# Second expert stage: weighted rows added into the output by an accumulating scatter

## What is computed

```python
x = x + 0.5 * ffn(layernorm(x), gate_w, gate_up_w, down_w)
x = x + mamba(layernorm(x), ...)
x = x + 0.5 * ffn(layernorm(x), gate_w, gate_up_w, down_w)
# ffn: 8 experts, F = 512, the 2 best of each token
probs = softmax(x @ gate_w.T); topw, sel = top_k(probs, 2); topw = topw / sum(topw)
out = sum over the 2 experts e of topw[e] * ((up_e(x) * gelu(gate_e(x))) @ down_e.T)
```

## Time and profile before

| | |
|---|---|
| three timed runs | 457.85, 460.02, 460.93 us; median 460.02 |
| span of the profiled execution | 459.4 us |
| PE busy | 404.0 us, 88% |
| DVE, ACT, POOL busy | 307.4, 240.0, 277.8 us |
| get: issue on POOL; issue to landing (median) | 1034 ns; 2.6 us |
| put: issue on POOL; issue to landing (median) | 1024 ns; 2.3 us |
| granted clock of TensorE, 328 to 441 us | 1.00 of full speed |

### The profile page before, as it was taken

How to read it: one execution, slowest core, us unless ns; L and a number is a source line. 1 busy time by engine, 2 the same in 40 slices (tenths; PEclk the granted TensorE clock), 3 DMA queues, 4 the chain that set the end, 5 groups by cost and what they waited for, 6 DMA issues and landing times.

```text
span 459.4 us, 9998 instructions
## 1 busy us (share of the span) xinstructions
PE 404.0 (88%) x2636; PEld 316.4 (69%) x2637; DVE 307.4 (67%) x761; ACT 240.0 (52%) x575; POOL 277.8 (60%) x262
## 2 busy tenths in 40 slices
PE   8779999999995998989979889984799999999940
PEld 6359999999994343434335346671499999999930
DVE  4824555555554967999989999999455555555516
ACT  4535444444434656686765867434454444444404
POOL 2167777777433252688685787765377777776330
PEclk9769999999997799999979999987699999999985
DMA  7942111112103200000000000001111111112026
GB/s 262 374 158 82 49 50 45 45 44 44 31 21 93 93 0 0 2 0 1 0 0 0 0 1 0 1 1 53 57 53 44 47 44 51 45 44 37 22 55 227
DMA packets 11964, 25.03 MB, mean 54 GB/s; under 512 B 3485, under 2 KB 4260, under 8 KB 11936
## 3 DMA queue, kind: packets, MB, share of 16 engines
q1 hardware_dynamic: 6944, 15.38, 9.5%
q0 software_dynamic: 4992, 9.32, 7.4%
HBM read 17.34 MB, written 8.26 MB: 56 GB/s over the span
## 4 chain that ended last, share of the span: by engine, by line
PE 65%; DVE 13%; ACT 7%; DMA 5%; issue 4%; POOL 4%; SPq 0%; POOLq 0%; ACTq 0%; DVEq 0%
PE ps L835 30%; PE ps L860 15%; PE ps L970 7%; DVE ring_space L1344 3%; DMA ring_space<-expert_rows 2%; ACT shared L705 2%; DVE stats L1097 2%; PE ps L830 2%; ACT ps L697 2%; POOL shared L486 2%; PE ps L957 2%; PE ps L951 2%; PE ps L903 1%; DMA xg<-xn_rows,get_i 1%; POOL rstd L398 1%
## 5 line engine op out<-in xcount | busy, mean ns | idle before, releaser
L835 PE MATMUL ps<-xT,w_now 128*128 128x128 f32 x1248 | 154.1, 277 | 0.8 <-ACT xT L574 0.7
L835 PEld LDWEIGHTS ps<-xT,w_now 128*128 128x128 f32 x1248 | 147.3, 194 | 1.4 <-ACT xT L574 1.1
L1226 DVE TENSOR_TENSOR hidden<-ps,hidden 128x256 f32<-128x256 f32 x156 | 58.9, 419 | 94.6 <-PE ps L835 94.6
L591 ACT ACTIVATE hidden<-ps 128x256 f32<-128x256 f32 x156 | 51.4, 381 | 111.2 <-PE ps L835 111.1
L434 POOL DMA_INDIRECT expert_rows<-ysb,put_i x78 | 79.9, 1024 | 46.5 <-DVE ysb L1234 30.1
L426 POOL DMA_INDIRECT xg<-xn_rows,get_i x78 | 80.6, 1034 | 45.1 <-issue 21.2
L486 POOL TENSOR_TENSOR shared<-ring_space,shared 128x512 f32<-128x512 f32 x64 | 81.9, 1287 | 35.5 <-DVE ring_space L1344 29.6
L860 PE MATMUL ps<-w_down,hidden 128*128 x624 | 82.1, 275 | 0.0
L970 PE MATMUL ps<-shared,consts 128*128 128x512 f32 x128 | 71.7, 644 | 7.6 <-POOL shared L486 7.4
L860 PEld LDWEIGHTS ps<-w_down,hidden 128*128 128x128 f32 x624 | 75.7, 192 | 0.2
L705 ACT COPY shared<-ps 128x512 f32<-128x512 f32 x64 | 37.6, 587 | 35.5 <-DVE ring_space L1344 18.2
(11 more groups left out here) (161 smaller groups left out, 410.6 us busy)
## 6 DMA issues: line engine op xcount, KB each, us to landing
w_gate_up<-in_experts SPq DMA_DIRECT2D x8, 512.0 KB, 8.6
xn_rows<-xn SPq DMA_DIRECT2D x8, 256.0 KB, 4.0
w_down<-in_experts SPq DMA_DIRECT2D x1, 2048.0 KB, 11.9
ring_space<-expert_rows SPq DMA_DIRECT2D x4, 512.0 KB, 5.9
xg<-xn_rows,get_i POOLq DMA_INDIRECT x78, 2.6
expert_rows<-ysb,put_i POOLq DMA_INDIRECT x78, 2.3
x<-in_x_rows SPq DMA_DIRECT2D x4, 256.0 KB, 4.5
ring_space<-expert_rows SPq DMA_DIRECT2D x4, 256.0 KB, 3.5
```

The lines of the kernel that those rows point to most:

```text
L591: nc.scalar.activation(gelu[:, slot % 2, half], ps[:, GATE_BANK[slot % 2], half], ACT.Gelu).then_inc(gelu_done, 1)
L835: m = pe.matmul(ps[:, bank, f * P:(f + 1) * P], w_now[:, slot % W_SLOTS, first + f * P:first + (f + 1) * P], xT[:, slot % X_SLOTS, :], sta ...
L1226: dve.tensor_tensor(hact[:, slot % H_SLOTS, half], ps[:, UP_BANK[slot % 2], half], gelu[:, slot % 2, half], ALU.mult).then_inc(hact_done, 1)
```

## The change

In the second stage alone:

- x after the Mamba block is stored at once to `out` (four stores on SP), which has grown to 7040 rows: the 2048 tokens, then one spare row for each of the 39 * 128 slots.
- The stored normalised rows have 130 columns instead of 128 (`xw`, `ROW`): columns 128 and 129 are the token's two weights. POOL makes `ldiff` group by group and the weights in two halves (`weights`), ACT runs its Exp in two halves, and SP waits for a half's weights before it stores the half's two groups. `normalise(2, 3)` comes after `row_ids(1)` and the second Exp.
- get(t) brings the weights with the rows and waits for `take_weight(t - 6)`, a new DVE instruction after `h_act`, which picks the row's weight into `slot_w`. `y_copy` multiplies by it.
- put(t) is an accumulating scatter into `out`. Filling rows go to their spare rows.
- A token may stand in two tiles of different experts, so puts are held apart: SP (`allow_puts`) lets put(t) go when `y_copy(t)` is done, the scatter of tile t - 2 has landed and, where tile t begins an expert, that of tile t - 1 has too. put(t) follows get(t + 8) instead of get(t + 10).
- DVE makes `add_i`, `not_second` and `starts_i` (`add_index`, eight instructions) ahead of its tile steps.
- The load of `expert_rows`, the scaling, the two additions and the six stores of x at the end of the second stage are gone. The first stage keeps them.

```diff
-PUT_AFTER = RING + TURN_AHEAD + DOWN_AFTER
+PUT_AFTER = RING + TURN_AHEAD + DOWN_AFTER, RING + DOWN_AFTER
+ROW = D + TOPK
+OUT_ROWS = T + NT * P
...
+            def landed(t):
+                return 16 * (PER_SLOT[t % RING] + t // RING + 1)
+            def allow_puts():
+                sp.wait_ge(add_index_ready, 1)
+                sp.wait_ge(base_stored, 16 * GROUPS)
+                for t in range(NT):
+                    if t >= 1:
+                        start = sp.value_load(starts_i[0:1, t:t + 1], min_val=0, max_val=16)
+                    sp.wait_ge(y_ready, NT + t + 1)
+                    if t >= 2:
+                        sp.wait_ge(scattered[(t - 2) % RING], landed(t - 2))
+                    if t >= 1:
+                        sp.wait_ge(scattered[(t - 1) % RING], start + (landed(t - 1) - 16))
+                    sp.sem_inc(may_put, 1)
...
+                        sp.wait_ge(out_added, g + 1)
+                        sp.dma_start(out[0:T].rearrange("(p c) d -> p c d", p=P)[:, grp(g), :], x[:, grp(g), :]
+                                     ).then_inc(base_stored, 16)
...
+                    if l:
+                        sp.wait_ge(weights_ready, g // 2 + 1)
+                    sp.dma_start(rows[:, grp(g), :], (xn, xw)[l][:, grp(g), :]).then_inc(xn_stored[g], 16)
...
+            def weights(h):
+                v = slice(2 * h * GC, 2 * (h + 1) * GC)
+                pool.wait_ge(e2_ready, h + 2)
+                chain(pool.tensor_scalar(den[:, v], e2[:, v], 1.0, None, ALU.add))
+                chain(pool.tensor_tensor(den[:, v], den[:, v], neg_one[:, v], ALU.pow))
+                chain(pool.tensor_tensor(xw[:, v, D], halves[:, v], den[:, v], ALU.mult))
+                pool.tensor_tensor(xw[:, v, D + 1], xw[:, v, D], e2[:, v], ALU.mult
+                                   ).then_inc(weights_ready, 1)
...
+                    if t >= RING and l == 1:
+                        pool.wait_ge(weight_taken, t - RING + 1)
...
+                    if l:
+                        pool.wait_ge(may_put, t + 1)
+                        pool.indirect_dma_start(
+                            out=out, in_=ysb[:, t % RING, :], in_offset=None,
+                            out_offset=bass.IndirectOffsetOnAxis(ap=add_i[:, t:t + 1].bitcast(U32), axis=0),
+                            bounds_check=OUT_ROWS - 1, oob_is_err=True, compute_op=ALU.add
+                            ).then_inc(scattered[t % RING], 16)
+                        return
...
+                dve.scalar_tensor_tensor(out=slot_w[:, slot % UNROLL:slot % UNROLL + 1], in0=row[:, D + 1:D + 2],
+                                             scalar=not_second[:, at], in1=row[:, D:D + 1],
+                                             op0=ALU.max, op1=ALU.min).then_inc(weight_taken, 1)
...
-            for i in range(len(PIECES[1])):
-                add_experts(1, i)
```

More of the change, by code:

```diff
@@ L233, in macaron_block @@
         get_i = sb("get_i", [P, NT], I32)
+        token = sb("token", [P, NT], I32)
+        second = sb("second", [P, NT], I32)
+        beyond = sb("beyond", [P, NT])
+        add_i = sb("add_i", [P, NT], I32)
+        not_second = sb("not_second", [P, NT])
+        at_start = sb("at_start", [P, NT, E])
+        starts = sb("starts", [P, NT])
+        starts_i = sb("starts_i", [P, NT], I32)
+        slot_w = sb("slot_w", [P, UNROLL])
         le_end = sb("le_end", [P, NT, E])
@@ L404, in mean_shift, with difference @@
                 pool.tensor_tensor(shift[:, v], neg_mean[:, v], rstd[:, v], ALU.mult).then_inc(shift_ready, groups)
+            def difference(g):
+                if g == 0:
+                    pool.wait_ge(diff_ready, 1)
+                pool.tensor_tensor(ldiff[:, grp(g)], ldiff_raw[:, grp(g)], rstd[:, grp(g)], ALU.mult
+                                   ).then_inc(ldiff_ready, 1)
+            def weights(h):
[6 more added lines that the diff above has]
+                                   ).then_inc(weights_ready, 1)
             def rsqrt_y(g):
@@ L443, in ffn @@
                     get(t)
[L444 removed]
+                for t in range(RING, NT + PUT_AFTER[l]):
                     if t < NT:
                         get(t)
[L447 to L448 removed]
+                    if t >= PUT_AFTER[l]:
+                        put(t - PUT_AFTER[l])
             def mamba():
@@ L512, in _ @@
                 mean_shift(2, g)
+                difference(g)
+                if g % 2:
+                    weights(g // 2)
             ffn(1)
@@ L527, in normalise @@
                 act.wait_ge(shift_ready, (GROUPS if s else 0) + g + 1)
-                if s:
-                    act.wait_ge(xn_stored[g], 16)
                 for c in range(g * GC, (g + 1) * GC):
-                    i = nc.scalar.activation(xn[:, c, :], x[:, c, :], ACT.Identity, bias=shift[:, c:c + 1],
+                    i = nc.scalar.activation((xw if s else xn)[:, c, 0:D], x[:, c, :], ACT.Identity, bias=shift[:, c:c + 1],
                                              scale=rstd[:, c:c + 1])
@@ L561, in row_ids, with second_weight @@
                 nc.scalar.activation(ids_rhs[:, 1], in_tile[:], ACT.Copy, scale=consts[:, K_P:K_P + 1]).then_inc(rows_ready, 1)
-            def second_weight(l):
-                act.wait_ge(ldiff_ready, l + 1)
-                nc.scalar.activation(e2[:], ldiff[:], ACT.Exp).then_inc(e2_ready, 1)
+            def second_weight(n, chunks):
+                act.wait_ge(ldiff_ready, n)
+                nc.scalar.activation(e2[:, chunks], ldiff[:, chunks], ACT.Exp).then_inc(e2_ready, 1)
             def ffn(l):
@@ L1183, in route, with add_index, second_weights @@
                 dve.tensor_scalar(weights_i[:], exp_f[:], float(E - 1), None, ALU.min).then_inc(experts_ready, 1)
-            def second_weights(l):
-                dve.wait_ge(e2_ready, l + 1)
+            def add_index():
+                chain(dve.tensor_scalar(second[:], put_i[:], 1, None, ALU.bitwise_and))
+                dve.tensor_scalar(not_second[:], second[:], -ABOVE_ONE, ABOVE_ONE, ALU.mult, ALU.add)
+                dve.scalar_tensor_tensor(out=beyond[:], in0=put_i[:], scalar=float(J * P),
+                                         in1=consts[:, K_SLOT:K_SLOT + NT], op0=ALU.is_ge, op1=ALU.mult)
+                chain(dve.tensor_scalar(token[:], put_i[:], 1, None, ALU.logical_shift_right))
+                dve.tensor_tensor(add_i[:], token[:], beyond[:], ALU.add)
+                chain(dve.tensor_tensor(at_start[:], spread(consts[:, K_TILE:K_TILE + NT], 2, [P, NT, E]),
+                                        spread(base[:], 1, [P, NT, E]), ALU.is_equal))
+                chain(dve.tensor_reduce(starts[:], at_start[:], AX.X, ALU.max))
+                dve.tensor_scalar(starts_i[:], starts[:], 16.0, None, ALU.mult).then_inc(add_index_ready, 1)
+            def second_weights():
+                dve.wait_ge(e2_ready, 1)
                 chain(dve.tensor_scalar(den[:], e2[:], 1.0, None, ALU.add))
@@ L1239, in step @@
                     h_act(i, slot)
+                    if l:
+                        take_weight(i, slot)
                     for lag in lags_of_step(i):
```

140 lines of the change are left out of this document (80 added, 60 removed).

## The result

| | before | after |
|---|---|---|
| median of the timed runs | 459.91 us (457.85 to 460.93) | 475.83 us (474.58 to 477.49) |
| span of the profiled execution | 459.4 us | 473.0 us |
| first get of the second stage | 328.04 | 325.02 |
| from there to the last put | 114.4 | 141.35 |
| from the last put's start to the end | 17.0 | 6.6 |

The changed kernel is slower, by a ratio of 1.0361 (95% interval 1.0323 to 1.0398). The last three rows split the profiled 13.6 us: -3.0 ahead of the first get, +26.95 between the first get and the last put, -10.3 behind it. The prediction had 116.7 us for the middle stretch (445.9 less 329.2) and about 3.5 behind the last put's start. So the end gave 10.3 us of the 13.5 that were forecast, and the body gave it back more than twice over.

A forecast was written before the change was run, and what follows sets the result against it. The prediction took PE to bound the kernel, with POOL close behind and a serial end. It summed 459.4 - 14.5 + 0.15 + 1.1 + 2.0 + 1.2 = 449.35, set to 450.0 us, range 445 to 468.

The forecast's parts named there:

- What bounds the kernel, and the end: PE bounds the second stage's body; behind its last landing 14.9 us run serially, of which 14.5 are removed.
- 0.4 us for what follows the last landing: End of program: the time kept from the last DMA's landing to the end, read from the last store.
- (a): End of the second stage: the last put starts later, being released through SP and following the put before, +0.15 us.
- (b): Last put's landing: the accumulating form lands in 3.2 us against 2.09, +1.1 us.
- (c): Issue of each put on POOL: 1.02 us for the accumulating form, bounded above at 1.53.
- Issue dear: Rival: at an issue of 1.53 POOL's pair takes 3.17 us and the time is 468; decides from about 1.3; chance 0.12.
- The body: puts held apart: Second stage's tiles: two-tile waits free up to a landing of 4.7; seven expert starts leave the last put 2.0 us late.
- 0.6 won back between starts: POOL in the body: of 1.45 us lateness per expert start, 0.6 is regained at 0.13 a tile before the next.
- 5.7 of slack of the gets: Gathers in the body: their lead over PE's need is 5.7 us, so PE loses 0.3 at most.
- Other work in the body: DVE's weight step and scaled copy, SP's register load, filling rows and longer gathered rows in the body: no cost.
- The head: Ahead of the second stage's first get: later weights delay the last stores, so the get starts at 329.2, +1.2 us.
- The sum: Whole kernel: all terms together give 449.35, set to 450.0 us, 2.2% below the kernel before.

The follow-up runs named there:

- e2_nosep: The changed kernel, still accumulating, but each slot adds into its own spare row and no put waits for another: 463.24 us, ratio 1.0066.
- e3_plain_nosep: The changed kernel with plain instead of accumulating puts, into rows of their own, none held back for another: 451.82 us, ratio 0.9801.
- e1_plain: The changed kernel with the second stage's scatter plain instead of accumulating, every wait, index and order kept: 450.77 us, ratio 0.9814.

## Right and wrong, point by point

**What bounds the kernel, and the end.** Right that the end was serial and could be removed: from the last put's start it went from 17.0 to 6.6 us. **Of the end, 0.4 us for what follows the last landing: wrong, it is 3.4.** The last put lands at 466.37 + 3.2 = 469.6 at the earliest, and the span ends at 473.0. POOL's queue at the end of the program (duration, start), after and before:

```profile
L142 POOLq DRAIN  x1: 6587/6587/6587, 466.1 to 466.1; - x1
```

```profile
L139 POOLq DRAIN  x1: 5922/5922/5922, 442.0 to 442.0; - x1
```

POOL's closing drain ends at 472.7, 3.1 us after that. Before, it ended at 447.9 and lay hidden behind the additions; the row was there to be read, and the term that was removed should have been 11.5, not 14.5.

**(a) The last put's start.** Right in the piece that it rests on: from SP's release of an idle POOL to its put there are 0.8 us, as in the earlier trace rows. The chain of waits, after, shows one:

```profile
461.47 0.02 SPq L379
...
462.26 1.07 POOL out_rows L495
```

**(b) The landing.** Right: 3.4 against 3.2, within 0.2, in all kernels whose puts all accumulate 128 rows (medians 3.3 to 3.4).

**(c) The issue on POOL: the step that failed.** 1.59 instead of 1.02, above even the upper bound of 1.53. It was argued from 0.98 with and without rows. Those rows say that the issue of a plain put does not depend on whether its rows are written. They cannot say what another form costs, and that was the question. The Trainium skill's page DMA: Bandwidth & Descriptors (Anatomy of one DMA — SWDGE (gpsimd) path) has many descriptors emitted before their cost shows; the runs agree in so far as 64 rows fewer save only 0.14 us of 1.59, but they speak against carrying that over to another form, 0.57 us dearer at equal rows.

With the pair at 3.25 instead of 2.66, the prediction's own rival *Issue dear*, which had a chance of 0.12, holds: e2_nosep against e3_plain_nosep shows 11.2 us in the body for it. That it would decide from an issue of about 1.3 fits: the body grows from a pair of about 2.96, which is an issue of 1.3. Its time, 468, was too low, by the 3.0 behind the last landing and by a body that had 19.3 us for issue and starts together, where the runs show 24.3; the first get, in the profile of after 4.2 us ahead of the forecast 329.2, takes some of that back.

**The body: puts held apart.** The two-tile chain is free, as said, while POOL has a reserve; the starts are the tiles named, at a distance of 4.1 to 4.5 in four of seven. What failed with (c) is the credit: 0.6 won back between starts and 5.7 of slack of the gets both come out of POOL's reserve and the delay that it builds up. Without reserve nothing is won back. The slack itself was sized about right (6.7 us by the trace of after, 9.3 at tile 8 less a landing of 2.6), but it is spent within the first three starts: PE's first long wait for a gather, 2.4 us, ends at 392.04. From there PE pays each start. With plain puts the step holds: e1_plain loses nothing by the waits, and after a start its puts come at 2.67 to 2.69, so 0.1 a tile is won back. That is no full test of it, since at a landing of 2.3 its starts take 3.2 and not 4.1.

**Other work in the body.** Right: `take_weight` and the longer `y_copy` cost nothing that shows, e1_plain's body equals that of before (114.5 against 114.4). `add_index` runs beside the first gets. "SP was idle" was true of the work, but its lateness at tile 32 had no place in the sum.

**The head.** Right, to 0.1 us. From the second group's `shift` to the first get there were 328.04 - 314.82 = 13.2 us; after, by POOL's timeline:

```profile
310.60 0.38 POOL L446 TENSOR_TENSOR shift<-neg_mean,rstd 128x4 f32<-128x4 f32 x1
...
318.93 1.72 POOL L460 TENSOR_TENSOR den<-den,neg_one 128x8 f32<-128x8 f32 x1
...
325.02 1.17 POOL L487 DMA_INDIRECT xg<-xn_rows,get_i  x1 [3.79 <-DMA xn_rows<-xw]
```

14.4 us, so +1.2, and the stores release the get, as said; all eleven kernels with this head have 14.4. The second half's pow, on which both stores hang, starts 8.3 us into the stretch, and by the prediction's times it would at about 8.4. That the stretch began 4.2 us earlier (310.60 against 314.82) comes from ahead of every edit, and lies within the 4 us over which the same head scatters.

**The sum, mended.** With 3.0 for the drain, the issue (11.2 in the body) and the waits (13.1 instead of 2.0) the forecast of 450.0 becomes 475.3; measured 475.8. These terms come from the runs that they explain, and the first get scatters by 4 us, so that the fit is this close is in part luck. The form and its waits took 24 us, more than the end was worth. Against the kernel before, e1_plain (0.9814) is what the rest of the change is worth, and no version that accumulates all 128 rows of every tile was faster than before: even without any wait e2_nosep is at 1.0066.

## What to carry to other kernels

Ask of every changed instruction whether the trace holds its very form; if not, price the engine that issues it by a range wide enough to cross the nearest bound, here 0.13 us of reserve on POOL against an unknown issue. The lead of the gathers hides a small excess (here up to a pair of about 2.96 against PE's 2.79), not one of 0.46 over 31 tiles. A wait that delays an engine is cheap only as long as that engine has reserve to win it back, so waits and a dearer issue must be priced together, not each by itself. When the work at the end is removed, look for what it covered: a closing drain that starts early in the trace will then be waited for.

## What the runs showed of the hardware

An accumulating indirect DMA of 128 rows of 512 bytes holds POOL for 1.59 us, a plain one for 1.02 to 1.04; with 64 rows it is still 1.44. This is not a queue that is backed up: put 32 of the kernel after starts when POOL has been idle for 4.68 us and the put before has landed, and takes 1.55. It lands in 3.4 us (64 rows: 3.0), a plain one in 2.3. It makes 144 packets, one per row and 16 more (64 rows: 80), where a plain one makes 32, and twice the busy share of the DMA engines did not slow the gathers: their median landing is 2.6 in the kernel after as in that before, and 2.7 in e1_plain and e2_nosep alike. TensorE's granted clock in the first tiles behind its wait for the gather differed between profiled executions with the same head, 0.50 for some 6 us in some, full in others, which moves the first put by up to 2.9 us. The closing drain of POOL ends about 3 us after the last of its DMAs has landed.
